# Value products of two key tiles back to back in two attention stages of a twelve-stage decoder

## What is computed

```
# memory attention (stage 7): 8 heads of 16, keys and values from the context
logits = einsum('bhqd,bhkd->bhqk', Q * depth**-0.5, K) + b[0] + -1e30 * (1 - mask)
out = einsum('bhqk,bhkd->bhqd', softmax(logits), V)          # k = 1601

# cross-self attention (stage 10): 16 heads of 8, context keys before the tokens' own
k = concat([extra_k, k]);  v = concat([extra_v, v])          # 1601 + 256 keys
attn = softmax(einsum('bhnd,bhmd->bhnm', q * scale, k))
out = einsum('bhnm,bhmd->bhnd', attn, v) @ w_proj.T + b_proj
```

## Time and profile before

| | |
|---|---|
| median of 3 runs | 5069.64 us (5061.39 to 5078.28) |
| span of the profiled execution | 5066.8 us |
| TensorE busy | 4085.0 us, 81% |
| VectorE busy | 3485.7 us, 69% |
| ScalarE busy | 2507.2 us, 49% |
| exponentials of both stages (L2452) | 688, 703.3 us busy |
| reductions of even looks (L2470) | 576, 564.9 us busy, 185.3 us idle before them |
| value products (L2396) | 5504 records, 436.2 us busy |
| mean granted TensorE clock | 0.883 |

### The profile page before, as it was taken

How to read it: one execution, slowest core, us unless ns; L and a number is a source line. 1 busy time by engine, 2 the same in 40 slices (tenths; PEclk the granted TensorE clock), 3 DMA queues, 4 the chain that set the end, 5 groups by cost and what they waited for, 6 DMA issues and landing times. The chain is left out here.

```text
span 5066.8 us, 77700 instructions
## 1 busy us (share of the span) xinstructions
PE 4085.0 (81%) x29323; PEld 2224.5 (44%) x29323; DVE 3485.7 (69%) x5453; ACT 2507.2 (49%) x3544; POOL 1378.9 (27%) x1033
## 2 busy tenths in 40 slices
PE   5640696999999999999995995866996767888883
PEld 3630234666666666666652332432443332222232
DVE  5579444777777777777784445766773558888868
ACT  2120243666666666666662223543564344677772
POOL 0000300566666666666664303000000100000000
PEclk5565798999999999999997996987997687999996
DMA  0010001000000000000003106316650333323300
GB/s 19 1 60 0 0 0 51 1 14 1 14 1 14 14 1 14 1 14 1 1 1 130 58 0 150 53 15 102 84 77 4 90 59 62 55 48 53 49 3 9
DMA packets 135603, 167.70 MB, mean 33 GB/s; under 512 B 19498, under 2 KB 108092, under 8 KB 134676
## 3 DMA queue, kind: packets, MB, share of 16 engines
q1 hardware_dynamic: 127540, 146.39, 14.3%
q0 software_dynamic: 6528, 16.42, 1.3%
q10 hardware_dynamic: 1184, 0.12, 0.0%
HBM read 125.31 MB, written 34.55 MB: 32 GB/s over the span
## 5 line engine op out<-in xcount | busy, mean ns | idle before, releaser
L3001 POOL TENSOR_TENSOR arena<-arena 128x512 f32<-128x512 f32 (+1 forms) x768 | 1131.7, 1475 | 692.0 <-ACT arena L2957 638.6
L2452 ACT ACTIVATE arena<-ps 128x1024 f32<-128x1024 f32 (+1 forms) x688 | 703.3, 1023 | 333.7 <-PE ps L2377 323.0
L2470 DVE TENSOR_REDUCE arena<-ps 128x2 f32<-128x826 f32 (+1 forms) x576 | 564.9, 981 | 185.3 <-PE ps L2323 177.5
L3017 DVE TENSOR_TENSOR arena<-arena 128x1024 f32<-128x1024 f32 (+1 forms) x448 | 644.9, 1478 | 13.8 <-ACT arena L2984 13.8
L3039 DVE TENSOR_TENSOR arena<-ps,arena 128x512 f32<-128x512 f32 (+1 forms) x768 | 530.4, 691 | 178.5 <-ACT arena L2951 144.4
L2323 PE MATMUL ps<-arena 48*128 48x413 bf16 (+3 forms) x1920 | 436.4, 334 | 135.9 <-DVE arena L2470 67.2
L2951 ACT ACTIVATE arena<-ps 128x1024 f32<-128x1024 f32 (+1 forms) x448 | 410.3, 960 | 205.1 <-PE ps L2879 197.0
L2863 PE MATMUL ps<-arena 128*128 128x256 f32 (+1 forms) x1664 | 444.0, 392 | 20.5 <-DVE arena L3025 19.2
L2957 ACT ACTIVATE arena<-arena 128x1024 f32<-128x1024 f32 (+1 forms) x448 | 425.0, 992 | 50.7 <-DVE arena L3017 48.2
L2396 PE MATMUL ps<-arena 128*9 128x256 f32 (+2 forms) x5504 | 436.2, 389 | 10.5 <-ACT arena L2440 7.7
L2879 PE MATMUL ps<-arena 64*128 64x256 f32 (+1 forms) x3328 | 427.3, 391 | 5.5 <-ACT arena L2973 1.3
(11 more groups left out here) (647 smaller groups left out, 5810.8 us busy)
## 6 DMA issues: line engine op xcount, KB each, us to landing
arena<-ctx_parts SPq DMA_DIRECT2D x96, 200.1 KB
arena<-ctx_parts SPq DMA_DIRECT2D x192, 100.1 KB
arena<-in_ctx_feat SPq DMA_DIRECT2D x8, 1601.0 KB, 6.4
arena<-in_ctx SPq DMA_DIRECT2D x16, 768.0 KB
arena<-diff_att_stack SPq DMA_DIRECT2D x60, 192.0 KB
ctx_parts<-arena SPq DMA_DIRECT2D x24, 400.2 KB, 3.8
arena<-in_w SPq DMA_DIRECT2D x1, 6416.0 KB, 18.3
arena<-in_ctx_feat SPq DMA_DIRECT2D x8, 800.5 KB
```

What stands on the lines that cost most here:

```text
L2452: act.activation(self.prob[0:rows, u % 3, :], self.ps[0:rows, 2 * (u % 2):2 * (u % 2) + 2, :].rearrange("p n c -> p (n c)"), ACT.Exp).then ...
L2470: ins = dve.tensor_reduce(dst[:, :, j // 2], self.ps[:, 4:6, 0:hi - lo], AX.X, ALU.max)
L3001: pool.tensor_tensor(acc[0:rows, u % 2, :], before, sc[0:rows, u % 2, t, :], ALU.add).then_inc(added, 1)
L3017: dve.tensor_tensor(e, e, mb[0:rows, u % 2, None, :].to_broadcast([rows, n, 2 * S]), ALU.subtract).then_inc(sub_done, 1)
```

## The change

The value products of steps are taken in pairs. In step t of a group, for even t from 2 on, TensorE issues the values of u-2 and u-1 one after the other; in odd steps it issues none. In step 0 it issues what is left of the group before (13 and 15 steps are both odd, so that is the last step alone). `prob` gets four slots for three, and the exponential of step u waits for the values of u-4 and no longer u-3. In stage 10 the small tile `rest_qk`, used only before the attention begins, is laid over the first two slots of `prob`.

```diff
-        self.prob = st.sb("prob", [P, 3, 4 * S])
+        self.ring = 4
+        self.prob = st.sb("prob", [P, self.ring, 4 * S])
...
+    def last_values(self):
+
+        return range((self.steps - 1) // 2 * 2, self.steps)
...
-                            self.prob[0:rows, u % 3, k % 2 * 2 * S + k // 2 * S:k % 2 * 2 * S + k // 2 * S + S],
+                            self.prob[0:rows, u % self.ring, k % 2 * 2 * S + k // 2 * S:k % 2 * 2 * S + k // 2 * S + S],
...
-            if u:
+            t = u % self.steps
+            if u and t == 0:
+                for v in self.last_values():
+                    self.pe_values(pe, u - self.steps + v)
+            elif t and t % 2 == 0:
+                self.pe_values(pe, u - 2)
                 self.pe_values(pe, u - 1)
...
-        self.pe_values(pe, total - 1)
+        for v in self.last_values():
+            self.pe_values(pe, total - self.steps + v)
...
-            if u >= 3:
-                act.wait_ge(s["pv_done"], u - 2)
+            if u >= self.ring:
+                act.wait_ge(s["pv_done"], u - self.ring + 1)
...
-            act.activation(self.prob[0:rows, u % 3, :], self.ps[0:rows, 2 * (u % 2):2 * (u % 2) + 2, :].rearrange(
+            act.activation(self.prob[0:rows, u % self.ring, :], self.ps[0:rows, 2 * (u % 2):2 * (u % 2) + 2, :].rearrange(
...
-            rest_qk = sa.sb("rest_qk", [P, 4, BANK])
+            rest_qk = att.prob[:, 0:2, :].rearrange("p r (h c) -> p (r h) c", c=BANK)
```

## The result

The changed kernel takes 5100.24 us (median of 4 runs, 5096.02 to 5104.14) against 5068.27 for the kernel before (4 runs, 5061.39 to 5078.28): ratio 1.0067, 95% interval 1.005 to 1.0083. It is slower by 0.7%, 32 us. The forecast was 5109 and slower. The code lines moved: looks are L2324 now, scores L2378, values L2401, exponentials L2463, reductions of even looks L2481, of odd ones L2484 and L2488, splits L2495, the divide after a turn back L2513 and L2514.

A forecast was written before the change was run, and what follows sets the result against it. It took TensorE's order (1.56 us) and VectorE's loop through banks 4,5 (1.47) as competing bounds, pairs starving VectorE. Memory +18, cross-self +25 and DMA waits -4 gave +39 us: 5109 us on the median, range 5066 to 5140.

The forecast's parts named there:

- Bound: Memory attention: TensorE's instruction order (1.56 us) and the loop through banks 4,5 (1.47) compete, within 0.09 us of each other.
- The fourth slot at zero: Exponentials waiting for the values of u-4 gain no wait, and laying `rest_qk` over two slots adds none: zero.
- The pair at 0.99: TensorE: two value groups in sequence take 0.43 + 0.56 = 0.99 us, the fixed part paid once; 0.21 saved per pair.
- (c): Rival: each value group pays its own fixed part, 0.13 more at five exposed pairs a group, +29 us, 5138; chance 0.10.
- Memory attention, +1.26 a group: Memory attention: exposed pairs cost more than intervals without values give back, +1.26 us on 14.5 groups, +18 us.
- The interval of the turn back: Memory attention, after the turn back in step 2: without values the next even look comes at +2.16, was +2.81: -0.65 us.
- Cross-self attention, +0.83 a group: Cross-self attention: seven pairs, some exposed and some hidden, less what short intervals give back: +0.83 us on 30.5 groups, +25 us.
- steps 14 to 0: Cross-self attention: a fully exposed pair between even looks, +0.49 us a group.
- Stalls outside the pattern, -4: Cross-self attention, nine groups: step 0's wait for the DMA of the maxima shrinks by about half a us each, -4.
- (a): Rival: TensorE is the bound and the pair saves it, -67 us, 5003, more likely half, 5036; chance 0.13.
- (b): Rival: two thirds of both stages' 43 us vanish in waits at split, turn back and maxima, +10, 5080; chance 0.13.
- (d): Rival: 0.55 us idle in odd steps lets the clock fall to 1.2 GHz more often, +36 on top, 5145; chance 0.06.

The follow-up runs named there:

- e6_short_pairs: The changed kernel with every reduction of a look reading 64 columns in place of 356 or 413: 4961.35 us, ratio 0.9799 to the kernel before.
- e1_four_slots: The changed kernel with four slots and `rest_qk` over two of them, but values one step behind as before: 5064.03 us, ratio 1.001 to the kernel before.
- memory alone: The changed kernel with pairs in the memory attention only, the cross-self attention taking one step at a time: 5083.43 us, ratio 1.0043 to the kernel before.
- cross-self alone: The changed kernel with pairs in the cross-self attention only, the memory attention taking one step at a time: 5077.13 us, ratio 1.0034 to the kernel before.
- e7_reordered: The kernel before, memory attention only: maxima's transposition moved into step 10, values ahead of the waiting look in step 3: 5035.65 us, ratio 0.9953.
- e5_short_single: The kernel before with every reduction of a look reading 64 columns in place of 356 or 413: 4994.95 us, ratio 0.9874.
- e8_reordered_pairs: The kernel before with the maxima's transposition moved into step 10, four slots and pairs in the memory attention alone: 5072.39 us, ratio 1.0018.

## Why the prediction was right

**Bound.** The two loops within 0.09 us of each other, TensorE's order at 1.56 and the loop through banks 4 and 5 at 1.47, were the key. The changed kernel shows both: 1.47 where nothing stands between even looks, 1.99 behind a pair. `e6_short_pairs` shows that with a short loop on VectorE the pair gains in the memory attention what the first loop alone allows (1.30 us a group against 1.26). In the cross-self attention other waits take its place.

**The fourth slot at zero.** Right by `e1_four_slots`.

**The pair at 0.99.** Measured 0.99, so the fixed part is paid once a pair and rival (c) is out. The weight loads of the pair, in the changed kernel's timeline:

```profile
3609.31 0.56 PEld L2401 LDWEIGHTS ps<-arena 128*17 128x17 f32 x16 [0.25 <-issue]
3610.30 0.11 PEld L2324 LDWEIGHTS ps<-arena 99*128 99x128 bf16 x2 [0.42 <-DVE arena L2484]
```

All sixteen are done at 3609.87, 0.43 before the next product starts, and all use 128 rows: the second step's loads run beside products of the same rows. The Trainium skill (TensorE: Matmul & The Clock Gate, Part 3) says in its list of what overlaps that loads do so only in other row groups; here the measurement decides against that. The same section also lets a load into the background weight buffer run ahead, which the prediction left out; the trace does not name the buffer, but it agrees with that. Its rule of the drain at a change of tiling mode (TensorEngine Tiling (Array Packing), Key Properties) fits the 0.99. The next load, for a look, comes only 0.43 after the last of them.

**Memory attention, +1.26 a group.** Measured +1.37. The single intervals came out within 0.02 of the forecast but for three. The interval of the turn back gave 2.28 between reductions (3610.81 to 3613.09): 0.52 less than the 2.80 it was, not 0.65, since the even reduction queues behind the odd one on VectorE. The one after it lost 0.34 and not 0.43, for the same reason. The split hid all but 0.08 of its pair, forecast 0.03.

**Cross-self attention, +0.83 a group.** Measured +0.89. The two intervals of 1.97 shown above are steps 9 to 10, which were 1.88 (+0.09, forecast +0.07), and steps 11 to 13, which were 1.47 (+0.50, forecast +0.49). The other one forecast at +0.49, steps 14 to 0, went from 1.88 to 2.32, +0.44.

**Stalls outside the pattern, -4.** This is the term that was mis-sized. The groups alone make 1.37 x 14.5 + 0.89 x 30.5 = 47 us, and the medians differ by 32, so about 15 us came back where the sum had 4. The runs of one stage say where: memory alone cost 0.26 to 0.60%, 13 to 30 us, where its groups make 20; cross-self alone 0.23 to 0.45%, 12 to 23 us, where its groups make 27. So at least 4 us, and perhaps 15, came back in the cross-self attention.

In the profiled executions, against 15 x 22.40 and 31 x 21.46 the kernel before has 6.2 and 25.6 us of other time between its first and last splits; the changed one has, against 15 x 23.77 and 31 x 22.35, 1.5 and 14.2. Most of it lies in groups with a lowered clock. Two neighbouring intervals between splits of the kernel before, columns as in the earlier trace rows:

```profile
3582.82:3609.32 26.50, 23.47 (x201) 10.29 (x200) 18.86 (x32) 13.84 (x16) 1.70 (x2) 0.87 0.47 58
3609.32:3631.72 22.40, 20.82 (x201) 9.69 (x200) 17.44 (x32) 13.84 (x16) 0.00 (x0) 1.00 0.70 103
```

The first, in which the granted clock is 0.87, is 4.1 us longer; it holds the stretch at 0.50 of the earlier trace rows. In the kernel before 7 of the 46 intervals have a mean granted clock of 0.59 to 0.93, and they hold 24.3 of the 31.8 us; in the changed one it is 5 intervals (0.57 to 0.93) and 13.9 of 15.7. How many there are differs between executions without any pair there: in the cross-self attention 2 in `e1_four_slots` and 6 in `e7_reordered`, and the remainder is 10.0 and 22.5 us. So the traces, one execution each, cannot size the term. The waits that it was made for, step 0 behind the DMA of the maxima, went from 13.2 to 6.2 us of weight loads' waiting, but it is 6.6 in `e1_four_slots`; what else came back stays open. The forecast of 5109 was 9 us over the median mostly by this term. The two group terms erred the other way, by 4 us together, so that part of the nearness is luck.

**Sign and rivals.** (a) needed VectorE not to run dry, and `e5_short_single` and `e6_short_pairs` show that the sign is the other one when its reductions are short. (b), delays taken up at split, turn back and maxima, did not happen in the repeated pattern beyond the pairs that I had counted as hidden; of what came back outside it only the part above is known. `e8_reordered_pairs` agrees with the reverse: the wait in step 3, where the pair gave 0.52 back, lowered the price of the pair. (d) did not happen: the clock of the two stretches is unchanged, and fewer intervals show it lowered.

**What I said too loosely.** TensorE's busy time fell by 43 us on the page, not some 50; the values alone fell by 60.

## What to carry to other kernels

An instruction that fills an engine's wait has a place, and its place is worth more than its cost. Before joining work to save switches, look at what the engine does in the spot that the work leaves: here 0.21 us a pair was saved and about 0.55 us of waiting opened in the odd step, since the even looks have one pair of banks and each waits for VectorE to finish the last. Whether a second pair of banks would let the pair of values pay was not tried; shorter reductions did. Where an engine waits for another at a fixed spot of each period, first move independent work into that spot; two such moves gave 0.5% here, and the pair took 0.7%. And where groups differ in length, ask for the granted clock of each before looking for a wait.

## What was unexpected of the hardware

Two float32 value groups in the same four column strips, sixteen matmul records, follow each other with no gap that the trace shows: 0.99 us at the full clock, exactly 0.43 + 0.56, with 0.43 worked out beforehand from one group at the two clock levels. And the schedule repeats to within 0.01 us: of the 15 split intervals of the changed kernel in the memory attention nine are 23.77, two 23.76, and four hold a stall of at most 0.5.
